# Second stage of the last groups: reordered on all engines, attention fused in 32x32 head tiles, outputs shared with ScalarE

## The reference, cut to what matters

```
x = x + dilated_attention(group_norm(x))        # first stage: 3x3 neighbourhoods, 4 dilations, gated
x = x + channel_attention(group_norm(x))        # second stage

channel_attention(e):                            # per image, 4 heads of 32 channels, n = 256 pixels
    p   = W_qkv @ e + b_qkv                      # 128 x 256
    att = softmax(p_h @ p_h.T / 16)              # per head h, 32 x 32
    out = W_proj @ concat_h(att_h @ p_h) + b_proj
```

## Time and profile before

| | us |
|---|---|
| median of 3 runs | 84.58 |
| the runs | 83.46 to 85.2 |
| the profiled execution, whole | 84.48 |
| its span, first to last instruction | 82.7 |
| busy in the span: PE / DVE | 68.7 / 68.5 |
| busy in the span: POOL / ACT | 40.3 / 30.2 |

### The profile page before, as it was taken

The page is one execution under the profiler, slowest core; times in us unless marked ns, Lnnn a source line. Parts: engine busy times, 40 slices in busy tenths (PEclk is TensorE's granted clock), DMA queues, the critical chain, the costliest instruction groups (busy, mean ns, idle before and its releaser), DMA issues.

```text
span 82.7 us, 2227 instructions
## 1 busy us (share of the span) xinstructions
PE 68.7 (83%) x888; PEld 52.0 (63%) x888; DVE 68.5 (83%) x191; ACT 30.2 (37%) x97; POOL 40.3 (49%) x82
## 2 busy tenths in 40 slices
PE   0099999979995699899969797879999787999960
PEld 0099899647981367677758664567685545667830
DVE  1087639999999989999999699889999999857980
ACT  4395539934376000000030003220993155485320
POOL 7104273005910027999999999699990003300000
PEclk9999999999999999999999999999999999999999
DMA  1895000300000000000000000000000000011244
GB/s 17 300 367 142 0 0 13 91 0 0 8 4 0 0 12 0 0 0 0 4 8 0 0 0 0 0 8 0 0 0 0 0 8 4 0 63 64 70 157 161
DMA packets 3019, 3.11 MB, mean 38 GB/s; under 512 B 320, under 2 KB 2752, under 8 KB 3008
## 3 DMA queue, kind: packets, MB, share of 16 engines
q1 hardware_dynamic: 2576, 2.69, 9.8%
q10 hardware_dynamic: 432, 0.26, 1.3%
HBM read 1.91 MB, written 1.05 MB: 36 GB/s over the span
## 4 chain that ended last, share of the span: by engine, by line
DVE 37%; POOL 28%; PE 21%; DMA 4%; issue 4%; ACT 2%; POOLq 1%
PE ps L762 19%; DVE qk L570 15%; POOL acc L339 14%; POOL pv L339 11%; DVE pv L611 4%; DMA xt<-x_dram 4%; DVE acc L623 4%; DVE pv L623 3%; POOL rstd L304 3%; DVE x L630 2%; PE ps L897 1%; DVE x L656 1%; ACT pT L400 1%; POOLq L99 1%; DVE prob L590 1%
## 5 line engine op out<-in xcount | busy, mean ns | idle before, releaser
L762 PE MATMUL ps<-prob,sel 64*128 64x192 f32 (+6 forms) x192 | 17.8, 313 | 2.7 <-DVE pv L611 1.6
L611 DVE TENSOR_TENSOR pv<-ps,v 128x128 f32<-128x128 f32 (+7 forms) x32 | 17.1, 569 | 1.8 <-PE ps L762 0.8
L762 PE MATMUL ps<-xn,wp 128*32 128x256 f32 (+1 forms) x208 | 18.1, 419 | 0.1
L762 PEld LDWEIGHTS ps<-prob,sel 64*128 64x128 f32 x192 | 13.6, 186 | 6.9 <-DVE pv L611 3.5
L570 DVE TENSOR_TENSOR qk<-q,k 128x720 f32<-128x720 f32 (+7 forms) x24 | 13.9, 642 | 1.0 <-ACT k L384 1.0
L762 PEld LDWEIGHTS ps<-xn,wp 128*32 128x32 f32 (+1 forms) x208 | 12.5, 126 | 3.3 <-ACT xn L407 0.8
L339 POOL TENSOR_TENSOR pv<-pv 128x240 f32<-128x240 f32 (+3 forms) x24 | 14.1, 599 | 0.5 <-DVE pv L611 0.5
L762 PE MATMUL ps<-xt 128*128 128x128 f32 x56 | 10.9, 342 | 4.0 <-DMA xt<-x_dram 4.0
L339 POOL TENSOR_TENSOR acc<-acc,pv 128x256 f32<-128x256 f32 (+4 forms) x20 | 12.7, 639 | 0.5
L304 POOL TENSOR_TENSOR rstd<-gvar,mhalf 128x2 f32<-128x2 f32 (+1 forms) x6 | 4.9, 823 | 15.3 <-DVE gvar L514 15.3
L762 PEld LDWEIGHTS ps<-xt 128*128 128x128 f32 x56 | 8.9, 235 | 5.2 <-DMA xt<-x_dram 4.0
(11 more groups left out here) (75 smaller groups left out, 91.3 us busy)
## 6 DMA issues: line engine op xcount, KB each, us to landing
xt<-x_dram SPq DMA_DIRECT2D x4, 256.0 KB, 3.6
out_dram<-x SPq DMA_DIRECT2D x8, 128.0 KB, 1.8
wp<-wpack_dram SPq DMA_DIRECT2D x1, 325.0 KB, 4.8
sel<-selc_dram SPq DMA_DIRECT2D x4, 64.0 KB, 3.8
cs<-consts_dram ACTq DMA_DIRECT2D x1, 130.0 KB, 3.3
cs<-consts_dram ACTq DMA_DIRECT2D x2, 64.0 KB, 2.7
```

The costliest lines, as they stand in the source:

```text
L611: last = nc.vector.tensor_tensor(o, a, b, ALU.mult)
L762: return nc.tensor.matmul(o, w, m, start=start, stop=stop)
```

## The change

- ScalarE ends five outputs, (0,0), (0,1), (1,0), (1,1) and (3,1). For these `finish` first multiplies the identity with x1 into the bank (256 columns, two passes), then adds M @ p to it, and ScalarE adds the bias while it copies from PSUM. VectorE keeps (2,0), (2,1) and (3,0).
- `attention_divide` writes the normalised attention `anorm` (both images in one instruction, 128x64) in place of the two block matrices. `fuse` is four products of 32 rows, 32 columns and 128 moving columns, one for each head, on the diagonal 32x32 tiles of the array. The mask leaves the constants (516 columns become 388).
- VectorE copies pT of groups 2 and 3 and mT of (3,1). ScalarE takes the norm of (2,1).
- The order of the tail changes on VectorE, ScalarE and TensorE; on TensorE six keep_clock products are added around the two group_stats and before project_second(2,0).
- The output DMA of (3,1) is issued from ScalarE's queue, the other seven from SyncE's.

```
-NORM_ON_DVE = (2, 3)
+NORMS_ON_DVE = ((2, 0), (3, 0), (3, 1))
+OUT_ON_ACT = ((0, 0), (0, 1), (1, 0), (1, 1), (3, 1))
...
@@ SyncE
-            for n in range(B):
-                b = batch(n // GB, n % GB)
-                sp.wait_ge(out_ready, n + 1)
-                sp.dma_start(out[b], x1[:, b, :]).then_inc(out_stored, 16)
+            for n in range(B - 1):
+                g, i = divmod(n, GB)
+                if (g, i) in OUT_ON_ACT:
+                    sp.wait_ge(out_act_ready, OUT_ON_ACT.index((g, i)) + 1)
+                else:
+                    sp.wait_ge(out_ready, n - 2 * GB + 1)
+                sp.dma_start(out[batch(g, i)], x1[:, batch(g, i), :]).then_inc(out_stored, 16)
...
@@ ScalarE
+            def second_residual(g, i):
+                act.wait_ge(fin_ready, GB * g + i + 1)
+                nc.scalar.activation(x1[:, batch(g, i), :], ps[:, BANK[g] + i, 0:N], ACT.Identity,
+                                     bias=wp[:, W_BP:W_BP + 1]).then_inc(out_act_ready, 1)
...
             attention_exp(0)
+            attention_exp(1)
             squares(2)
-            attention_exp(1)
-            copy_fused(0, 0)
             squares(3)
-            copy_fused(0, 1), copy_fused(1, 0), copy_projection(2, 0..1), copy_fused(1, 1), copy_pT(2, 0..1),
-            copy_projection(3, 0..1), attention_exp(2), copy_pT(3, 0..1), copy_fused(2, 0), attention_exp(3),
-            copy_fused(2, 1), copy_fused(3, 0..1)
+            copy_fused(0, 0..1), norm(2, 1), copy_projection(2, 0..1), copy_projection(3, 0..1),
+            second_residual(0, 0..1), copy_fused(1, 0..1), attention_exp(2), attention_exp(3),
+            second_residual(1, 0..1), copy_fused(2, 0..1), copy_fused(3, 0), second_residual(3, 1)
+            act.wait_ge(out_act_ready, len(OUT_ON_ACT))
+            act.dma_start(out[batch(3, 1)], x1[:, batch(3, 1), :]).then_inc(out_stored, 16)
...
@@ VectorE, attention_divide
-                for i in range(GB):
-                    nc.vector.scalar_tensor_tensor(out=ablk[:, g, i, :].rearrange("p (h e) -> p h e", h=H1),
-                                                   ..., op0=ALU.mult, op1=ALU.mult).then_inc(ablk_ready, 1)
+                nc.vector.tensor_tensor(anorm[:, g], aex[:, g], view(arec, GB * g, [[1, GB], [0, HD1]]),
+                                        ALU.mult).then_inc(anorm_ready, 1)
...
@@ VectorE, the order from attention_shift(1) on
+            first_residual(2), first_residual(3), second_variance(2), attention_divide(0), second_variance(3),
+            second_norm_bias(2), norm(2, 0), second_norm_bias(3), norm(3, 0..1), copy_pT(2, 0..1),
+            attention_divide(1), copy_pT(3, 0..1), attention_shift(2), attention_shift(3),
+            attention_divide(2), attention_divide(3), second_residual(2, 0), copy_fused(3, 1),
+            second_residual(2, 1), second_residual(3, 0)
...
@@ TensorE
+                for h in range(H1):                                              # fuse
+                    rows = slice(HD1 * h, HD1 * h + HD1)
+                    last = mm(ps[rows, BANK[g] + i, 0:P], anorm[rows, g, i, :], wp[rows, W_PT:W_PT + P])
...
+                if on_act:                                                       # finish, behind its wait
+                    mm(ps[:, BANK[g] + i, 0:N], ident, x1[:, batch(g, i), :], stop=False)
+                mm(ps[:, BANK[g] + i, 0:N], mT[:, g, i, :], p1[:, g, i, :], start=not on_act).then_inc(fin_ready, 1)
...
@@ TensorE, the order behind restore(3)
+            wait ashift_ready 2, keep_clock(2), group_stats(2), keep_clock(3), group_stats(3), fuse(0, 0..1),
+            keep_clock(1), project_second(2, 0..1), finish(0, 0), project_second(3, 0), transpose(2, 0),
+            project_second(3, 1), transpose(2, 1), finish(0, 1), transpose(3, 0), attention(2),
+            transpose(3, 1), fuse(1, 0..1), attention(3), finish(1, 0..1), fuse(2, 0..1), fuse(3, 0..1),
+            finish(2, 0..1), finish(3, 0..1)
```

More of the change, by code:

```diff
@@ L157, in build @@
         arec = sb("arec", [P, GROUPS, GB])
-        ablk = sb("ablk", [P, GROUPS, GB, P])
+        anorm = sb("anorm", [P, GROUPS, GB, HD1])
         mT = sb("mT", [P, GROUPS, GB, P])
@@ L213, in build @@
         pT_copied = sem("pT_copied")
+        pT_dve_copied = sem("pT_dve_copied")
         att_ready = sem("att_ready")
@@ L216, in build @@
         aexp_ready = sem("aexp_ready")
-        ablk_ready = sem("ablk_ready")
+        anorm_ready = sem("anorm_ready")
         mT_ready = sem("mT_ready")
         mT_copied = sem("mT_copied")
+        mT_dve_copied = sem("mT_dve_copied")
         p1_ready = sem("p1_ready")
@@ L223, in build @@
         out_ready = sem("out_ready")
+        out_act_ready = sem("out_act_ready")
         out_stored = sem("out_stored")
@@ L466, in _ @@
             attention_exp(0)
+            attention_exp(1)
             squares(2)
-            attention_exp(1)
-            copy_fused(0, 0)
             squares(3)
-            copy_fused(0, 1)
-            copy_fused(1, 0)
             for i in range(2):
-                copy_projection(2, i)
-            copy_fused(1, 1)
+                copy_fused(0, i)
+            norm(2, 1)
+            for g in range(2, 4):
+                for i in range(2):
+                    copy_projection(g, i)
             for i in range(2):
-                copy_pT(2, i)
+                second_residual(0, i)
             for i in range(2):
-                copy_projection(3, i)
+                copy_fused(1, i)
             attention_exp(2)
+            attention_exp(3)
             for i in range(2):
[L482 to L485, removed]
+                second_residual(1, i)
             for i in range(2):
-                copy_fused(3, i)
+                copy_fused(2, i)
+            copy_fused(3, 0)
+            second_residual(3, 1)
+            act.wait_ge(out_act_ready, len(OUT_ON_ACT))
+            act.dma_start(out[batch(3, 1)], x1[:, batch(3, 1), :]).then_inc(out_stored, 16)
         @block.vector
@@ L645, in attention_divide, with copy_pT, copy_fused @@
                 link(nc.vector.reciprocal(arec[:, g], asum[:, g]))
-                for i in range(GB):
-                    nc.vector.scalar_tensor_tensor(out=ablk[:, g, i, :].rearrange("p (h e) -> p h e", h=H1),
-                                                   in0=view(aex, (GB * g + i) * HD1, [[0, H1], [1, HD1]]),
-                                                   scalar=arec[:, g, i:i + 1], in1=view(cs, C_BLK, [[HD1, H1], [1, HD1]]),
-                                                   op0=ALU.mult, op1=ALU.mult).then_inc(ablk_ready, 1)
+                nc.vector.tensor_tensor(anorm[:, g], aex[:, g], view(arec, GB * g, [[1, GB], [0, HD1]]),
+                                        ALU.mult).then_inc(anorm_ready, 1)
+            def copy_pT(g, i):
+                dve.wait_ge(pT_ready, GB * g + i + 1)
+                nc.vector.tensor_copy(pT[:, g, 2 * i:2 * i + 2, :].rearrange("p a n -> p (a n)"),
+                                      ps[:, BANK[g] + i, 0:N]).then_inc(pT_dve_copied, 1)
+            def copy_fused(g, i):
+                dve.wait_ge(mT_ready, GB * g + i + 1)
+                nc.vector.tensor_copy(mT[:, g, i, :], ps[:, BANK[g] + i, 0:P]).then_inc(mT_dve_copied, 1)
             def second_residual(g, i):
@@ L734, in _ @@
             first_residual(2)
-            attention_divide(0)
             first_residual(3)
             second_variance(2)
-            attention_divide(1)
+            attention_divide(0)
+            second_variance(3)
             second_norm_bias(2)
-            second_variance(3)
-            for i in range(2):
-                norm(2, i)
+            norm(2, 0)
             second_norm_bias(3)
@@ L746, in _ @@
             for i in range(2):
-                second_residual(0, i)
+                copy_pT(2, i)
+            attention_divide(1)
+            for i in range(2):
+                copy_pT(3, i)
             attention_shift(2)
+            attention_shift(3)
             attention_divide(2)
-            attention_shift(3)
-            second_residual(1, 0)
             attention_divide(3)
[L753 to L757, removed]
+            second_residual(2, 0)
+            copy_fused(3, 1)
+            second_residual(2, 1)
+            second_residual(3, 0)
         @block.tensor
@@ L886, in project_second @@
             def project_second(g, i):
-                if g in NORM_ON_DVE:
-                    pe.wait_ge(xn1_ready, GB * (g - NORM_ON_DVE[0]) + i + 1)
+                if (g, i) in NORMS_ON_DVE:
+                    pe.wait_ge(xn1_ready, NORMS_ON_DVE.index((g, i)) + 1)
                 else:
-                    pe.wait_ge(xn1_act_ready, GB * g + i + 1)
+                    pe.wait_ge(xn1_act_ready, GB * g + i + 1 if g < 2 else 2 * GB + 1)
                 mm(ps[:, BANK[g] + i, 0:N], wp[:, W_1T:W_1T + P], xn1[:, g, i, :]).then_inc(p1_ready, 1)
@@ L903, in attention @@
                 for i in range(GB):
```

(54 more changed lines are left out.)

2 lines of the change are left out of this document (1 added, 1 removed).

## The result

| | kernel before | changed kernel |
|---|---|---|
| median of the first comparison (4 runs each) | 84.89 us | 87.05 us |
| ratio, 95% interval | | 1.027 [1.020, 1.034] |
| median of the second comparison (7 and 4 runs) | 83.80 us | 85.91 us |
| ratio, 95% interval | | 1.028 [1.022, 1.034] |
| tail, first pass of restore(2) to end of last matrix product | 14.33 us | 16.58 us |

They lift that median to 87.05; the ratios leave such runs out, and the two others took 86.16 and 86.05. The forecast was 86.3.

A forecast was written before the change was run, and what follows sets the result against it. The prediction took TensorE's queue from 71.60 us as the bound: the last output ends 1.97 us later, less 0.15, so +1.8 on 84.48 gives 86.3 us. Eight in ten: 84.5 to 87.8 us.

The forecast's parts named there:

- The early part: Statistics and norms of groups 2 and 3, ahead of TensorE's tail queue: group 3's norms end 0.97 us earlier.
- The queue: TensorE's issue time from 71.60: work waiting at every step, sum 9.15 us, reaching finish(3,1) at 80.75.
- return to full-size tiles: On TensorE in the tail: three returns each make the next pass some 0.05 us longer.
- correction made on it: 0.15 us taken off the 1.97 sum, because the same walk over the order before ended its last output 0.46 late.
- gap at a change of shape: TensorE tail: seven changes of tile shape at 0.1 us each, 0.70 in all; nothing as lower bound.
- The room: Tail from 71.2 to 79.94: products need 7.1 of 8.74 us, leaving about 1.6 us of TensorE waits.
- not-slower rival: Tail: identity passes fall into latencies, the tail keeps its length, group 3 starts 0.97 earlier; 83.5 us, chance 0.12.
- Rival three: Fusions on diagonal tiles run one behind another, +0.66 us each, 5.3 in all; 91.6 us, chance 0.07.
- full drain: TensorE at changes of tiling mode: would cost 0.165 us a change, making the sum 0.45 larger.
- The cover: VectorE's pT and anorm are ready 0.6 us before TensorE needs them, so its copies add nothing to the sum.
- DMA rival: End of the span: ScalarE's DMA queue is slow for the last output, +1.5 us; 87.8 us, chance 0.08.
- shorter-queue rival: TensorE tail: no gap at shape changes (-0.7), norm (2,1) on time (-0.4); +0.7 us, 85.2 us, chance 0.15.

The follow-up runs named there:

- no_identity: Changed kernel without the identity products of the five finishes, so x is not added there; tail 14.78 us, time 84.37 us, 1.012 of the kernel before.
- more_passes: Changed kernel with four further unread passes of 128 columns ahead of each of the five identity products; tail 18.82 us, time 87.98 us (one run).
- last_dma_sync: Changed kernel with the DMA of output (3,1) issued by SyncE; tail 16.58 us, time 88.00 us (one run, clock at half for 3.4 us).
- norm_on_vector: Changed kernel with the norm (2,1) on VectorE behind norm (2,0); tail 16.48 us, time 86.45 us (one run).
- before_identity: Kernel before with the five outputs on ScalarE behind identity products, otherwise its own orders and block matrix; tail 15.64 us, time 85.48 us, ratio 1.023.
- new_order: Kernel before with diagonal-tile fusions, no identity products, all outputs on VectorE and a reworked tail order; tail 13.97 us, time 83.63 us, ratio 0.998.
- changed_again: Changed kernel measured once more, unaltered, for a second trace; tail 16.58 us, time 85.91 us, ratio 1.028 against the kernel before.

## Why the prediction was right, point by point

- **The early part** came out right to 0.01, partly by luck: project_second(2,1) and the copies let the first finish begin 5.98 us after the first restore pass (70.98 - 65.00); the prediction had 71.60 - 65.61 = 5.99. Group 3's norms ended at 71.08, 6.08 after the restores, where the prediction had 6.09. In between, gvar(3) ended 0.09 later than predicted, and its rsqrt took 0.70 in place of 0.80. This gain of 1 us reached nobody, as argued.
- **The queue** was the right step and a little too small. Predicted from the first finish to finish(3,1): 80.79 - 71.60 = 9.19. Measured: 80.45 - 70.98 = 9.47. The last product took 1.12 (80.45 to 80.98 + 0.59), predicted 1.13. All three parts make 16.58.
- **The mis-sized term** is the return to full-size tiles together with the correction made on it. The gap at a change of shape was 0.10, as taken (77.44 + 2 x 0.215 = 77.87, and the fusions begin at 77.97). But behind it the first full-size products are longer: the pair at 76.04 took 0.70 in place of 0.59, the six passes at 78.97 took 1.56 in place of the 1.46 of the earlier trace rows, 0.10 each time, and a fusion pair takes 0.57 with its change of shape (75.08 to 75.65), not 0.54. That is most of the 0.28. The prediction named 0.05 for each of three returns, left it out of the sum, and then took 0.15 off the sum, because the same walk over the kernel before had ended late. That correction was wrong here. Perhaps the walk errs high where TensorE waits for others, and in the changed kernel it hardly waits (0.08 for mT(3,1), where the prediction had 0.05); no run shows this. The delay to the last product was 16.58 - 14.33 = 2.25; the sum said 1.97, the forecast 1.8.
- **The room** was counted short. The prediction has seven finishes behind 71.2; its rows show six, one at 75.06, three at 76.71 and two at 78.81. finish(0,1) lies ahead of them:

```profile
70.72 0.70 PE L762 MATMUL ps<-p,mT 128*128 128x256 f32 x2
71.25 1.84 PE L762 MATMUL ps<-xn,wp 128*128 128x256 f32 x6
```

  So the products need 6.7 us of the 8.74, and the room was 2.0, not 1.6. The sum of the queue does not use it, but the argument against the not-slower rival did, and 2.0 us of room for 2.15 of passes hardly speaks against it. What does is measured: only 0.84 vanished in the order of before, and 0.35 in the changed one.
- **The absolute time** came out near by luck, by two errors that cancel. The profiled execution from which I started, at 84.48, was itself long ahead of the tail (last section); most runs of the kernel before took 83.5 to 84.0. 83.8 + 2.25 is 86.05, and the changed kernel took 85.8 to 86.6 where its clock stayed up. 84.48 + 1.8 is 86.3.
- **Diagonal tiles** run side by side: a pair of fusions, 16 passes, took 0.64 (68.93), and one behind another they would take at least 16 x 0.11. Rival three is out. The rule of the Trainium skill (TensorEngine Tiling (Array Packing), Key Properties) that tiles operate independently agrees with that row, and its drain at a mode change with the 0.10 gap, though not with a full drain, which the prediction had worked out as 0.165.
- **The cover** on VectorE held for pT and anorm: TensorE's products did not wait for them in the queue. In no_identity, where the queue is shorter, it did wait for anorm(2), which is the cover named as 0.6 us. A pT copy on VectorE took 0.42; I had taken 0.37 between 0.28 and 0.48.
- **The not-slower rival** wanted TensorE idle for 2 us in the tail. It was not, and more_passes shows no slack at all. The DMA rival is out by last_dma_sync. The shorter-queue rival asked for no gap at shape changes, which are there with 0.10, and for a norm on time; that is worth 0.10 (norm_on_vector), not 0.4.
- Of the 2.25 us, 1.80 go with the identity products in the changed order. The remaining 0.45 (no_identity against before) is the order with everything else in it; norm_on_vector explains 0.10 of it. In no_identity's trace two waits can be named, 0.20 for anorm(2) and 0.18 ahead of the last product; how much of the other 0.35 they are, no run separates.

## What to carry to other kernels

Moving work off an engine gained nothing here, because that engine did not end the chain, and an add that is free on VectorE (the residual rode on the bias) is not free as an identity product: 0.43 us of TensorE each, 1.8 us of 2.15 in the end. Before such a trade, list every pass of the receiving engine in the stretch by its issue distance, not by its record, and set the sum against the waits in it: here 2.0 us of room for 2.15 of passes, of which the orders could use 0.84 and 0.35. And count products that keep the clock as part of the schedule: taking them out is an experiment, not a saving.

## What the runs showed of the hardware beyond this

**TensorE's clock makes the kernel's runs differ by 1 to 2 us.** Its first products run at the pace of the lower level, 1.2 GHz, and the moment at which it rises moves from run to run. The granted clock's column doesn't show this early part; the passes do. Where the column reads 0.50 (27.7 to 31.1 in the first trace of the changed kernel), a pass of the same projections lasts 634 ns, and 385 where it reads 1.00 in the second. Projections between 9.5 and 12 us, first in the kernel before (its profiled execution), then in no_identity:

```profile
L762 PE MATMUL ps<-xn,wp 128*32 128x256 f32 x28 | 3.6, 633 | 0.0
```

```profile
L782 PE MATMUL ps<-xn,wp 128*32 128x256 f32 x51 | 3.2, 381 | 0.0
```

The same code runs its products at 633 and at 381 ns, and puts 28 and 51 into the stretch. The restores of the tail began at 65.61 in the first and at 64.75 in the second. Other traces agree: 442 ns in before_identity and 419 in new_order go with 65.14 in both, 381 in changed_again with 65.00. Beside that, the clock sometimes fell to half in the first stage. The first trace of the changed kernel, from 24 us on, and below it the second trace:

```profile
24.00:27.70 3.70, 1.73 (x28) 0.48 (x20) 3.63 (x6) 1.77 (x5) 0.00 (x0) 1.00 0.00 0
27.70:31.10 3.40, 3.38 (x24) 1.74 (x24) 2.56 (x3) 0.00 (x0) 0.57 (x1) 0.50 0.04 7
```

```profile
24.00:27.70 3.70, 1.71 (x28) 0.71 (x22) 3.63 (x6) 1.47 (x5) 0.00 (x0) 1.00 0.00 0
27.70:31.10 3.40, 3.40 (x40) 2.27 (x40) 3.06 (x5) 0.00 (x0) 0.73 (x1) 1.00 0.03 7
```

TensorE was as little busy before it in both (1.73 and 1.71 of 3.70 us), and only one lost its clock; the restores began at 66.89 there and at 65.00 here. A part of these 1.9 us is a later rise of the clock (457 against 381 ns between 9.5 and 12 us). That stage is the same code in all kernels of this study, and the kernel before has such runs too (85.3 to 86.9, each with a mean clock of 0.98). Four others of its runs took 85.1 to 86.0 at a mean granted clock of 1.0; a late rise, which that mean does not show, would fit them, but they have no trace. A tail can be compared from single traces to about 0.1 us; a whole time here cannot, and 0.4% is under what the comparison with new_order can tell.
